# The q and k projection of an attention block: one fp32 product from x in place of three fp32r products from a split x

## The reference

```python
q = Wq @ x + bq          # 64 x 1024
k = Wk @ x + bk          # 64 x 1024
v = Wv @ x + bv          # 128 x 1024
attn = softmax(q.T @ k)  # 1024 x 1024, over the last axis
out = gamma * (v @ attn.T) + x
```

## Time and profile before

| what | value |
|---|---|
| median of 3 runs | 234.23 us |
| the profiled execution's own time | 234.46 us |
| its span | 232.6 us |
| PE busy (matmul), share of the span | 221.2 us, 95% |
| PE weight load | 189.2 us, 81% |
| POOL | 200.4 us, 86% |
| ACT | 179.3 us, 77% |
| DVE | 175.9 us, 76% |

### The profile page before, as it was taken

The page is one execution under the profiler, slowest core; times in us unless marked ns, Lnnn a source line. Parts: engine busy times, 40 slices in busy tenths (PEclk is TensorE's granted clock), DMA queues, the critical chain, the costliest instruction groups (busy, mean ns, idle before and its releaser), DMA issues.

```text
span 232.6 us, 4731 instructions
## 1 busy us (share of the span) xinstructions
PE 221.2 (95%) x1608; PEld 189.2 (81%) x1608; DVE 175.9 (76%) x289; ACT 179.3 (77%) x345; POOL 200.4 (86%) x174
## 2 busy tenths in 40 slices
PE   6997999999999999999999999999999999999981
PEld 5464988888788878889789988898798899899880
DVE  1687388796888877796978968797878969696374
ACT  2768887788688877789787886789777878788942
POOL 8688998589996899789996899968996998879990
PEclk9999999999999999999999999999999999999998
DMA  3637900670709325490527607192215803011002
GB/s 85 204 151 175 272 7 2 138 184 3 224 14 232 75 70 159 99 219 3 168 60 175 143 0 230 34 231 55 98 41 120 195 4 135 2 48 45 0 3 90
DMA packets 18023, 24.39 MB, mean 105 GB/s; under 512 B 9936, under 2 KB 10832, under 8 KB 18000
## 3 DMA queue, kind: packets, MB, share of 16 engines
q1 hardware_dynamic: 17552, 23.89, 39.6%
q10 hardware_dynamic: 448, 0.20, 0.3%
HBM read 8.59 MB, written 4.19 MB: 55 GB/s over the span
## 4 chain that ended last, share of the span: by engine, by line
POOL 56%; issue 24%; PE 11%; DVE 4%; ACT 1%; DMA 1%; POOLq 1%; ACTq 0%
POOL weight_lo L458 38%; POOL x_turned_sb L466 7%; POOL total L472 6%; POOL values_b L450 3%; POOL x_lo L439 3%; DVE neg_max L822 2%; PE sums L597 2%; PE work L541 2%; DMA w_qk<-in_L_conv_Wk 1%; PE scores L578 1%; PE scores L579 1%; PE scores L535 1%; PE sums L613 1%; PE scores L639 1%; PE sums L524 1%
## 5 line engine op out<-in xcount | busy, mean ns | idle before, releaser
L458 POOL TENSOR_TENSOR weight_lo<-weight,weight_hi 128x512 bf16<-128x512 f32 x90 | 122.9, 1387 | 21.0 <-ACT weight_hi L756 20.9
L822 DVE TENSOR_REDUCE neg_max<-work 128x1 f32<-128x512 f32 x120 | 80.8, 684 | 26.5 <-PE work L541 26.4
L753 ACT ACTIVATE weight<-scores 128x512 f32<-128x512 f32 x128 | 76.9, 601 | 19.4 <-PE scores L579 14.2
L597 PEld LDWEIGHTS sums<-values,weight_hi 128*128 128x128 f32 x504 | 77.2, 188 | 10.6 <-issue 0.5
L597 PE MATMUL sums<-values,weight_hi 128*128 128x258 f32 x504 | 80.6, 282 | 0.1
L756 ACT ACTIVATE weight_hi<-scores 128x512 fp32r<-128x512 f32 x128 | 77.0, 601 | 0.0
L578 PE MATMUL scores<-q_hihi,k_hilo 128*128 128x512 f32 x128 | 53.4, 417 | 0.7 <-ACT weight_hi L756 0.7
L541 PE MATMUL work<-k_hilo,q_hihi 128*128 128x512 f32 x120 | 48.6, 409 | 2.0 <-DVE neg_max L822 1.6
L579 PE MATMUL scores<-q_lomax,k_hione 128*128 128x512 f32 x128 | 50.4, 394 | 0.0
L853 DVE TENSOR_TENSOR weight_lo<-weight,weight_hi 128x512 bf16<-128x512 f32 x38 | 39.1, 1028 | 4.5 <-ACT weight_hi L756 4.5
L613 PE MATMUL sums<-values_b,weight_lo 128*128 128x130 bf16 x496 | 34.3, 221 | 0.0
(11 more groups left out here) (80 smaller groups left out, 162.3 us busy)
## 6 DMA issues: line engine op xcount, KB each, us to landing
x_turned_sb<-in_x_turned SPq DMA_DIRECT2D x8, 512.0 KB, 5.3
out<-y_sb SPq DMA_DIRECT2D x15, 256.0 KB, 2.5
x_sb<-in_x SPq DMA_DIRECT2D x7, 512.0 KB, 4.7
q_hihi<-qk_hi SPq DMA_DIRECT2D x12, 256.0 KB, 4.2
q_lomax<-qk_lo SPq DMA_DIRECT2D x7, 256.0 KB, 5.0
k_hione<-qk_hi SPq DMA_DIRECT2D x7, 256.0 KB, 5.0
k_hilo<-qk_hi SPq DMA_DIRECT2D x6, 256.0 KB, 3.1
k_hilo<-qk_lo SPq DMA_DIRECT2D x6, 256.0 KB, 5.0
```

The source lines that it names most:

```text
L458: pool.tensor_tensor(weight_lo[:, r], weight[:, r], weight_hi[:, r], ALU.subtract).then_inc(weight_lo_pool_done, 1)
L597: last = pe.matmul(sums[:, it, 0:VCOLS], weight_hi[:, r, tile(it)], values[p][:, j], start=(j == 0), stop=False)
L753: act.activation(weight[:, r], scores[:, s % 2], ACT.Exp)
L822: dve.reduce_max(neg_max[:, t, h:h + 1], place, AX.X, negate=True).then_inc(neg_max_done, 1)
```

## The change

`project_qk` issues, for every image from 1 on, the one plain fp32 product from x and the unsplit weights that only image 1 had. It waits for the DMA of x in place of the splits. The tiles x_hi, x_lo, w_qk_hi and w_qk_lo, the functions `round_x` and `rest_of_x`, the two weight splits and the three semaphores between them are gone.

```diff
@@ gpsimd
-            def rest_of_x(n, h):
-                pool.wait_ge(x_hi_done, half_count(n - 1, h))
-                if n > 2:
-                    pool.wait_ge(qk_done, half_count(n - 1, h))
-                pool.tensor_tensor(x_lo[:, chunk(h)], image(n)[:, chunk(h)], x_hi[:, chunk(h)],
-                                   ALU.subtract).then_inc(x_lo_done, 1)
...
-            pool.wait_ge(w_ready, 3)
-            pool.tensor_scalar(w_qk_hi[:, :], w_qk_t[:, :], 0.0, 1.0, ALU.add, ALU.mult).then_inc(w_split, 1)
-            pool.wait_ge(w_split, 1)
-            pool.tensor_tensor(w_qk_lo[:, :], w_qk_t[:, :], w_qk_hi[:, :], ALU.subtract).then_inc(w_split, 1)
...
-                if k in (4, 6) and b + 2 < BATCHES:
-                    rest_of_x(b + 2, (4, 6).index(k))
@@ tensor
             def project_qk(n, h, place):
-                if n == 1:
-                    wait_x(pe, n)
-                    last = pe.matmul(place, w_qk_t[:, :], image(n)[:, chunk(h)], start=True, stop=True)
-                else:
-                    pe.wait_ge(w_split, 2)
-                    pe.wait_ge(x_lo_done, half_count(n - 1, h))
-                    pe.matmul(place, w_qk_hi[:, :], x_hi[:, chunk(h)], start=True, stop=False)
-                    pe.matmul(place, w_qk_lo[:, :], x_hi[:, chunk(h)], start=False, stop=False)
-                    last = pe.matmul(place, w_qk_hi[:, :], x_lo[:, chunk(h)], start=False, stop=True)
-                last.then_inc(qk_done, 1)
+                wait_x(pe, n)
+                pe.matmul(place, w_qk_t[:, :], image(n)[:, chunk(h)], start=True, stop=True).then_inc(qk_done, 1)
@@ scalar
-            def round_x(n, h):
-                wait_x(act, n)
-                if n > 2:
-                    act.wait_ge(qk_done, half_count(n - 1, h))
-                act.activation(x_hi[:, chunk(h)], image(n)[:, chunk(h)], ACT.Copy).then_inc(x_hi_done, 1)
...
-                if k in (3, 5) and b + 2 < BATCHES:
-                    round_x(b + 2, (3, 5).index(k))
```

More of the change, by code:

```diff
@@ L148, in attention_program @@
         w_qk_t = sbuf("w_qk_t", [CHANNELS, 2 * HEAD], fp32)
-        w_qk_hi = sbuf("w_qk_hi", [CHANNELS, 2 * HEAD], fp32r)
-        w_qk_lo = sbuf("w_qk_lo", [CHANNELS, 2 * HEAD], fp32r)
         w_v_t = sbuf("w_v_t", [CHANNELS, CHANNELS], fp32)
@@ L163, in attention_program @@
         x_turned_sb = sbuf("x_turned_sb", [TILE, TURNED, TILES, CHANNELS], fp32)
-        x_hi = sbuf("x_hi", [CHANNELS, PIXELS], fp32r)
-        x_lo = sbuf("x_lo", [CHANNELS, PIXELS], fp32r)
         q_first = sbuf("q_first", [HEAD, HALVES, CHUNK], fp32)
@@ L205, in attention_program @@
         first_q_lo_done = sem("first_q_lo_done")
-        w_split = sem("w_split")
-        x_lo_done = sem("x_lo_done")
         first_v_lo_done = sem("first_v_lo_done")
@@ L229, in attention_program @@
         w_v_ready = sem("w_v_ready")
-        x_hi_done = sem("x_hi_done")
         qk_hi_done = sem("qk_hi_done")
```

## The result

The changed kernel takes 236.21 us, the median of 6 runs (235.73 to 237.11), beside 234.69 us of the kernel before (6 runs). The ratio is 1.0071, with a 95% interval of 1.0046 to 1.0095: slower by 1.5 us (1.1 to 2.2 by the interval), where 1.34 was forecast. The profiled execution took 236.27 us with a span of 234.5. Lines of the changed kernel: L502 projects q and k, L512 is the max product, L549 and L550 the scores, L784 the reduction, L839 the output half (L877 before), L815 VectorE's weight_lo (L853), L443 GpSimd's, L451 the bias (L466).

A forecast was written before the change was run, and what follows sets the result against it. TensorE's stream of products was taken to bound the kernel. Seven products at +0.17 us (1.19) plus 5 x 0.03 gave +1.34 us, so 235.6 us from the median of 234.23; range 233.4 to 237.3 us.

The forecast's parts named there:

- What bounds the kernel: TensorE's stream of products sets the time; another engine counts only where it makes that stream stop.
- The products: On TensorE, a plain fp32 product takes 0.86 us against 0.69 for three fp32r: +0.17 for each of 12.
- Where it is paid: k = 12 of six images and image 0's first product pay +1.19 us; five others hide in a 0.43 us pause.
- That VectorE would not come sooner: VectorE's reduction of k = 8 gains nothing from GpSimd's lighter list: +0.03 us for each of five images.
- the other outcome: Rival at VectorE's output half: VectorE is freed and TensorE's pauses go, -2.6 us, 231.6 us; 12%.
- The size: Whole kernel: 1.19 + 5 x 0.03 = +1.34 us, a median of 235.6 us.
- the sign that I had given for being wrong: Image windows over 27.4 us would mean a dearer product or a pause at a new place.
- PE waits for no DMA in that stretch now: Transfers of qk_hi and qk_lo, 0.17 us later at k = 12, first needed at next image's k = 2: no cost.
- Weight loads: Rival on TensorE: weight loads set the pace, so dropping one of three gives -2.3 us, 231.9 us; 4%.
- Nothing is hidden: Rival: the pause moves along with the product, so all 12 pay, +2.04 + 0.15, 236.4 us; 11%.
- 0.99: Rival: each fp32 product on TensorE takes 0.99 us, giving +2.45, 236.7 us; 9%.
- The lock falls worse: Rival: GpSimd's weight_lo of k = 9 starts just before VectorE's weight_lo asks, +3.0 us, 237.2 us; 5%.

The follow-up runs named there:

- keeping their work: Changed kernel with all products plain fp32, but ScalarE and GpSimd still making the unused splits and TensorE still waiting for them: ratio 1.0071, median 236.90 us.
- the second product alone: Kernel before with only each image's second q and k product (k = 12) plain fp32, the first still three fp32r products: 236.48 us, ratio 1.0057.
- the first alone: Kernel before with only each image's first q and k product (k = 8) plain fp32, the second still three fp32r products: 235.59 us, ratio 1.0026.
- kernel with the later bias: Changed kernel with GpSimd's bias moved from k = 7 to k = 8, behind the weight_lo of k = 9: 232.91 us, ratio 0.9905.
- kernel with the moved split: Kernel before with x_lo at k = 3 and 9, x_hi at k = 2 and 8, VectorE's weight_lo at k = 9 for 8: 230.55 us, ratio 0.9818.
- kernel before with `DVE_LOW` changed: Kernel before with one number changed, so VectorE makes the weight_lo of k = 9 in place of k = 8: median 234.73 us, ratio 0.9910.
- `DVE_LOW` in the changed kernel: Changed kernel with VectorE making the weight_lo of k = 9 in place of k = 8: 232.90 us, ratio 0.9913.
- the projection at k = 11: Changed kernel with GpSimd's bias at k = 8 and the second q and k product at k = 11 in place of 12: 234.05 us, ratio 0.9954.
- the held DMAs: Changed kernel with SyncE holding back the DMAs of q_lomax and k_hione until the four before them have landed: 237.88 us, ratio 1.0124.

## Why the prediction was right

- *What bounds the kernel.* Right. GpSimd lost 18 us of work and ScalarE 5, with no gain, and keeping their work left the windows of images 1, 2, 3 and 5 as they were. What gained time, 0.4 to 0.9 us an image, was in each kernel a pause of TensorE's stream that went.
- *The products.* 0.86 against 0.69, taken from four records at the start of the kernel, was right to 0.01 in the steady part. The estimate of +0.22 was too high, as the rows already said: 0.17 with 0.69 for three fp32r products. It was worked out from the four passes in the Trainium skill, "FP8 and Floating Point Precision" (TensorE Precision Notes).
- *Where it is paid.* Right and shown from both sides: the second product alone +0.18 in the window of image 3, the first alone 0.00.
- *That VectorE would not come sooner.* Right, and the step with the most risk. The image that already had the changed list of GpSimd gave 4.30 us for the reduction; it came at 4.28. The kernel with the later bias shows how near the other outcome was: L839 at 0.68, and 232.9 us.
- *The size.* +1.34 forecast. The two profiled executions are 1.8 apart (236.27 and 234.46), the medians 1.5. The profile shows 1.19 of products, under 0.1 and not 0.15 for the five hidden ones, and 0.8 of two pauses that the sum had at nothing. Image 4 even shows the sign that I had given for being wrong, a window over 27.4 with a pause at a new place. Both pauses lay in statements that I didn't check far enough. "PE waits for no DMA in that stretch now" is true of the earlier trace rows, but says nothing of how near a DMA comes or of how long it will take next time: the last of the four transfers had 1.0 us to spare and then took 2.7 longer, for a reason that stays open. And I worked out the order of VectorE against GpSimd for images 1 to 5 and took image 0 to be free of it. That the medians lie within 0.2 of the forecast in spite of 0.8 left out is therefore in part luck: their difference is known to some 0.6 us either way, and the products make up 1.2 of it.
- *The rivals.* Weight loads: one of three dropped and the stream slower, so they don't set the pace. "Nothing is hidden" falls by the windows of images 1, 2, 3 and 5 (+0.18, not +0.34), "0.99" by the 0.86 at k = 12. "The lock falls worse" falls by L815, 1.21 us in image 3 (1.17 before), though in image 0 the same lock did cost 0.2.

## What to carry to other kernels

Where one engine's stream sets the time, price an exchange in that stream only, from start to start of undisturbed records, and then look whether a pause stands next to it: the pause will swallow the cost, or hide the gain. Work taken off another engine was worth nothing here by its amount; what counted is which of its instructions is running when the critical chain asks, and a stretch of the same trace that already has the new order (here the image without a projection) answers this better than an argument does. A DMA that had landed in time took 2.7 us longer here after a change that leaves its instruction alone, so look at the slack of what isn't waited for, too. And before believing a cure, follow everything that moves up on every queue, for each of the three misses here (`DVE_LOW` in the changed kernel, the projection at k = 11, the held DMAs) came from an instruction that I had not followed.

## What the runs showed of the hardware

A tensor_tensor on VectorE with both operands in SBUF took 0.68 to 0.69 us where GpSimd ran nothing as it started, in all 21 cases of 128x512 in the kernel before, weight_lo and output halves together. In the other 32 it ended 0.45 to 0.65 us after the GpSimd instruction that was then running, and took up to 1.8. The 120 reductions from PSUM kept to 0.67 to 0.69 throughout. This is what the Trainium skill states in "SBUF — State Buffer" (SBUF: two separate sides): the two engines share a port pair under an exclusive lock for a whole instruction. The trace agrees, with 1.58 us for L839 behind a bias of 1.30, and 0.68 with GpSimd idle in the kernel with the later bias. Moving that one bias by a step took the ratio from 1.0071 to 0.9905. One wait can also last longer than one GpSimd instruction. In image 0 of the kernel with the moved split, GpSimd went from the bias (until 32.48) straight to a weight_lo (until 33.74), and L853, asked for at 31.86, ended only at 34.28; in image 0 of the kernel before with `DVE_LOW` changed, L853 took 4.86 us in the same way. In the first case TensorE stood for 0.5 us behind it.
